# Delta net weights loaded ahead and in parts, zero experts added last, indexed return of the GELU experts' rows

## The reference, cut to what matters

```
x = x + 0.5 * zero_moe(layernorm(x))      # stage 0: 8 routed experts of width 128 + 4 "zero" experts, top 2
x = x +       attention(layernorm(x))     # stage 1
x = x + 0.5 * zero_moe(layernorm(x))      # stage 2: as stage 0
x = x + 0.5 * gelu_moe(layernorm(x))      # stage 3: 8 experts of width 1024, top 2
x = x +       delta_net(layernorm(x))     # stage 4: gated delta rule, 16 key heads, 32 value heads of 128
x = x + 0.5 * gelu_moe(layernorm(x))      # stage 5: as stage 3

zero_moe:  out = sum_e w[e] * down_e(silu(gate_e x) * up_e x) + x * sum(w[zero experts])
gelu_moe:  out = sum over the two picks of w * (gelu(x W1_e + b1_e) W2_e + b2_e)
delta_net: qkvz = x W_qkvz; causal conv of 4 taps and silu on q, k, v; chunks of 64; ...; out = core W_out
```

## Time and profile before

| What | Value |
|---|---|
| median of three runs | 2405.76 us (2404.11 to 2411.33) |
| the profiled execution | 2403.5 us, its span 2401.8 us |
| TensorE busy | 2025.8 us, 84% |
| VectorE busy | 1286.1 us, 54% |
| ScalarE busy | 1000.3 us, 42% |
| GpSimd busy | 391.6 us, 16% |
| mean granted TensorE clock | 0.924 of full speed |

### The profile page before, as it was taken

How to read it: one execution, slowest core, us unless ns; L and a number is a source line. 1 busy time by engine, 2 the same in 40 slices (tenths; PEclk the granted TensorE clock), 3 DMA queues, 4 the chain that set the end, 5 groups by cost and what they waited for, 6 DMA issues and landing times. The chain is left out here.

```text
span 2401.8 us, 52328 instructions
## 1 busy us (share of the span) xinstructions
PE 2025.8 (84%) x20606; PEld 1490.4 (62%) x20606; DVE 1286.1 (54%) x2928; ACT 1000.3 (42%) x2476; POOL 391.6 (16%) x442
## 2 busy tenths in 40 slices
PE   7889898788626689999999999999999998858884
PEld 4544455677514467767776776777677667638774
DVE  4435444212234576777667767766776776431222
ACT  2114421222113445664665566556546654512221
POOL 0002100200200122212221222122122212202102
PEclk9969998899856899999999999999999999958997
DMA  1100003710101111011101110110111010045001
GB/s 46 33 13 1 15 26 105 250 31 21 44 11 45 30 31 24 18 35 24 33 20 37 24 33 20 33 27 18 35 24 33 20 28 11 11 164 187 27 21 62
DMA packets 148345, 100.08 MB, mean 42 GB/s; under 512 B 88640, under 2 KB 134992, under 8 KB 148112
## 3 DMA queue, kind: packets, MB, share of 16 engines
q1 hardware_dynamic: 144368, 86.59, 12.8%
q0 software_dynamic: 3744, 10.23, 1.5%
HBM read 83.28 MB, written 13.50 MB: 40 GB/s over the span
## 5 line engine op out<-in xcount | busy, mean ns | idle before, releaser
L1589 PE MATMUL dn_ps<-xnT,dn_w 128*128 128x512 f32 x512 | 260.5, 635 | 35.2 <-DMA dn_w<-in_W_qkvz_dram 23.9
L1942 DVE SCALAR_TENSOR_TENSOR dn_cv<-dn_raw,dn_cw,dn_cv 128x1024 f32<-128x1024 f32 x192 | 270.6, 1409 | 1.2
L588 PE MATMUL g_ps<-g_w,xnT 128*128 (+1 forms) x736 | 166.1, 379 | 0.0
L1589 PEld LDWEIGHTS dn_ps<-xnT,dn_w 128*128 128x128 f32 x512 | 91.2, 197 | 116.3 <-issue 100.1
L577 PE MATMUL g_ps<-g_xT,g_w_now 128*128 128x128 f32 x960 | 117.4, 282 | 50.3 <-DVE g_w_now L716 50.3
L1734 PE MATMUL dn_ps<-dn_wout,dn_oT 128*128 128x256 f32 x512 | 150.0, 418 | 6.2 <-ACT dn_oT L1749 3.7
L1749 ACT ACTIVATE dn_kdk<-dn_ps,dn_cf 128x128 f32<-128x128 f32 x256 | 80.2, 364 | 179.3 <-PE dn_ps L1629 179.3
L516 ACT ACTIVATE xnT<-g_ps,g_b_now 128x128 f32<-128x128 f32 x240 | 68.6, 368 | 206.1 <-PE g_ps L577 206.1
L577 PEld LDWEIGHTS g_ps<-g_xT,g_w_now 128*128 128x128 f32 x960 | 112.6, 196 | 61.5 <-issue 61.5
L588 PEld LDWEIGHTS g_ps<-g_w,xnT 128*128 128x128 f32 x736 | 136.4, 190 | 16.7
L1749 ACT ACTIVATE dn_raw<-dn_ps 128x512 f32<-128x512 f32 x128 | 76.6, 598 | 148.7 <-PE dn_ps L1589 148.7
(11 more groups left out here) (309 smaller groups left out, 4413.2 us busy)
## 6 DMA issues: line engine op xcount, KB each, us to landing
g_w<-in_fc_dram SPq DMA_DIRECT2D x32, 1024.0 KB, 13.1
dn_w<-in_W_qkvz_dram SPq DMA_DIRECT2D x16, 768.0 KB, 4.5
dn_x<-dn_cum_rows SPq DMA_DIRECT2D x32, 256.0 KB, 3.9
ys_rows<-g_ys SPq DMA_DIRECT2D x46, 128.0 KB, 1.7
dn_wout<-in_W_out_dram SPq DMA_DIRECT2D x16, 256.0 KB, 2.8
f_gate<-in_gateT_dram SPq DMA_DIRECT2D x16, 128.0 KB, 2.2
f_up<-in_upT_dram SPq DMA_DIRECT2D x16, 128.0 KB, 2.4
f_down<-in_downT_dram SPq DMA_DIRECT2D x16, 128.0 KB, 2.4
```

The costliest lines, as they stand in the source:

```text
L588: last = pe.matmul(y_b[i % 2][:, 0:D], hT[i % 2][:, f, :], of(f), start=(f == 0), stop=(f == NF - 1))
L1589: mm = pe.matmul(to, w[:, k, W_COL[u] * P:(W_COL[u] + 1) * P], m.xnT[:, k, b * T:(b + 1) * T], start=(k == 0), stop=(k == KD - 1))
L1942: ins = nc.vector.scalar_tensor_tensor(out=cv[:, u], in0=raw[:, u, :, tap:tap + T], scalar=cw[:, g, tap:tap + 1], in1=cv[:, u], op0=ALU.mu ...
```

## The change

1. `top_two`: the 8 MAX8 follow one another with one wait, then the 8 FIND_INDEX8 with one wait.
2. `moe_zero`: the 8 additions of `xn * zero_w` stand after the experts' loop.
3. `moe_gelu`: VectorE's loop has `copy_w1(i + 1)` first. The tile's result goes to `ys_rows` by an indirect DMA of GpSimd (`put_back`), each row straight to the row of its token and pick; all slots without a token go to one spare row, 2048. Each `put_back` waits for the one before to have landed. When all have landed, SyncE loads the rows back with 16 plain DMAs of 128 KB. `place_u` now comes out of the routing matmuls by a third column group of `token`. The four bias additions stand ahead of the sixteen additions.
4. `delta_net`: the first head's `w`, `cw`, `wout` and all constants are issued in the gates' stage (`load_first`); later heads' q, k and v columns (512 KB) are loaded once `proj` 7 of the head before is done, the z columns (256 KB) once `proj` 11 is.

```diff
@@ top_two
-        chain(nc.vector.max(m8[:, t, :], scores[:, t, :]))
-        chain(nc.vector.max_index(ix[:, t, :], m8[:, t, :], scores[:, t, :]))
+        nc.vector.max(m8[:, t, :], scores[:, t, :]).then_inc(chain.sem, 1)
+    chain.n += NT
+    chain.eng.wait_ge(chain.sem, chain.base + chain.n)
+    for t in range(NT):
+        nc.vector.max_index(ix[:, t, :], m8[:, t, :], scores[:, t, :]).then_inc(chain.sem, 1)
...
@@ moe_zero, vector
-            for t in range(NT):
-                nc.vector.scalar_tensor_tensor(out=m.x[:, t, :], in0=m.xn[:, t, :], scalar=zero_w[:, t:t + 1],
...
-            dve.wait_ge(chain_sem, chain.n + NT)
+            dve.wait_ge(chain_sem, chain.n)
...
+            dve.wait_ge(acc_done, 2 * UNITS * STEPS + A_FREE)
+            for t in range(NT):
+                nc.vector.scalar_tensor_tensor(out=m.x[:, t, :], in0=m.xn[:, t, :], scalar=zero_w[:, t:t + 1],
...
@@ moe_gelu, sync
-            for i in range(TILES):
-                sp.wait_ge(y_copied, i + 1)
-                sp.dma_start(tile_rows(ys_rows, i), ys[:, i % 3, :]).then_inc(ys_stored[i % 3], 16)
+            sp.wait_ge(y_copied, TILES)
             for n in range(3):
                 sp.wait_ge(ys_stored[n], 16 * ((TILES - n + 2) // 3))
+            for t in range(NT):
+                for r in range(2):
+                    sp.dma_start(gathered[r][:, t, :], tile_rows(ys_rows, r * NT + t)).then_inc(ys_back[t], 16)
@@ moe_gelu, gpsimd
+            def put_back(i):
+                pool.wait_ge(y_copied, i + 1)
+                if i >= 1:
+                    pool.wait_ge(ys_stored[(i - 1) % 3], 16 * ((i + 2) // 3))
+                nc.gpsimd.indirect_dma_start(ys_rows, bass.IndirectOffsetOnAxis(ap=place_u[:, i:i + 1], axis=0),
+                                             ys[:, i % 3, :], None).then_inc(ys_stored[i % 3], 16)
+
+            for i in range(RING):
+                fetch(i)
             pool.wait_ge(place_ready, 1)
...
+            for i in range(TILES):
+                if i + RING < TILES:
+                    fetch(i + RING)
+                put_back(i)
@@ moe_gelu, tensor and vector: routing
-            pe.wait_ge(token_ready, 2)
+            pe.wait_ge(token_ready, 3)
...
+            nc.vector.tensor_tensor(token[:, :, 2, :], in_tile[:], over_tiles(route[:, R_BACK:R_BACK + 2 * NT]), ALU.mult).then_inc(token_ready, 1)
...
-            chain(nc.vector.scalar_tensor_tensor(out=place_f[:], in0=tile_f[:], scalar=float(P), in1=slot[:], op0=ALU.mult, op1=ALU.add))
-            nc.vector.tensor_copy(place_u[:], place_f[:]).then_inc(place_ready, 1)
...
+            chain(nc.vector.scalar_tensor_tensor(out=place_f[:], in0=in_tile[:, 0, :], scalar=float(SPARE), in1=in_tile[:, 1, :],
+                                                 op0=ALU.add, op1=ALU.add))
+            nc.vector.tensor_tensor(place_u[:], place_f[:], in_tile[:, 2, :], ALU.subtract).then_inc(place_ready, 1)
@@ moe_gelu, vector: the loop
             for i in range(TILES):
+                if E1 <= i + 1 < TILES:
+                    copy_w1(i + 1)
                 if i + 2 < TILES:
                     copy_x(i + 2)
                 if i >= 1:
                     copy_y(i - 1)
-                if E1 <= i + 1 < TILES:
-                    copy_w1(i + 1)
             copy_y(TILES - 1)
@@ delta_gates, sync (behind its own loads)
+            first = load_first(sp, first_loaded)
...
+            sp.wait_ge(first_loaded, 16 * first)
@@ delta_net
+        def load_first(sp, first_loaded):
+            sp.dma_start(w[:], weights_of(0)).then_inc(first_loaded, 16)
+            sp.dma_start(cw[:], taps_of(0)).then_inc(first_loaded, 16)
+            sp.dma_start(wout[:], out_of(0)).then_inc(first_loaded, 16)
...
             def load_weights(kh):
+                wait(sp, "pj", kh * 12 - 4)
+                sp.dma_start(w[:, :, 0:4 * P], weights_of(kh)[:, :, 0:4 * P]).then_inc(w_loaded, 16)
+
+            def load_z_weights(kh):
                 wait(sp, "pj", kh * 12)
-                sp.dma_start(w[:], W_qkvz[:, kh * NCOL:(kh + 1) * NCOL].rearrange("(k p) n -> p k n", p=P)).then_inc(w_loaded, 16)
+                sp.dma_start(w[:, :, 4 * P:NCOL], weights_of(kh)[:, :, 4 * P:NCOL]).then_inc(wz_loaded, 16)
```

More of the change, by code:

```diff
@@ L342 @@
 R_PART, R_TILE = R_SLOT + P, R_SLOT + P + 1
-R_WIDTH = R_TILE + 2 * NT
+R_BACK = R_TILE + 2 * NT
+R_WIDTH = R_BACK + 2 * NT
+SPARE = 2 * NTOK
 def route_constants():
@@ L359, in route_constants @@
     tile = np.tile(P * np.arange(NT), 2).astype(np.float32)
+    back = (SPARE - NTOK * (np.arange(2 * NT) // NT)).astype(np.float32)
     spread = lambda a: np.broadcast_to(a, (P, len(a)))
     part = r[:, None].astype(np.float32)
-    return np.ascontiguousarray(np.concatenate([before, ones, groups, count, spread(rows), part, spread(tile)], axis=1))
+    return np.ascontiguousarray(np.concatenate([before, ones, groups, count, spread(rows), part, spread(tile), spread(back)], axis=1))
 def moe_gelu(nc, m, tag, gate, gate_bias, fc1, fc1_b, fc2, fc2_b, alpha, iota_in, route_in, xn_rows, ys_rows):
@@ L481, in _, with fetch @@
             pool.wait_ge(tokens_ready, 1)
-            for i in range(TILES):
+            def fetch(i):
                 if i >= RING:
@@ L544, in _ @@
                     pe.wait_ge(in_slot_ready, j // 4 + 1)
-                last = pe.matmul(y_b[0][:, 0:2 * TILES], in_slot[:, j, :], token[:, j].rearrange("p a n -> p (a n)"),
+                last = pe.matmul(y_b[0][:, 0:3 * TILES], in_slot[:, j, :], token[:, j].rearrange("p a n -> p (a n)"),
                                  start=(j == 0), stop=(j == 2 * NT - 1))
@@ L731, in _ @@
                     copy_y(i - 1)
-                if E1 <= i + 1 < TILES:
-                    copy_w1(i + 1)
             copy_y(TILES - 1)
+            for g in range(4):
+                dve.wait_ge(b2_ready, g + 1)
+                two = m.x[:, 2 * g:2 * g + 2, :].rearrange("p t d -> p (t d)")
+                nc.vector.tensor_tensor(two, two, h_b[g], ALU.add).then_inc(b2_added, 1)
             for t in range(NT):
-                if t % 2 == 0:
-                    dve.wait_ge(b2_ready, t // 2 + 1)
-                    two = m.x[:, t:t + 2, :].rearrange("p t d -> p (t d)")
-                    nc.vector.tensor_tensor(two, two, h_b[t // 2], ALU.add).then_inc(b2_added, 1)
                 dve.wait_ge(b2_added, t // 2 + 1)
@@ L1154, with delta_gates @@
 (K_BETA, K_NBETA, K_CUM, K_NGE, K_GE, K_KD, K_GL) = range(7)
-def delta_gates(nc, m, tag, W_ba, A_log, dt_bias, table, cf, cum_rows):
+def delta_gates(nc, m, tag, W_ba, A_log, dt_bias, table, cf, cum_rows, load_first):
     with ExitStack() as ctx:
@@ L1430, in delta_net @@
         w16, w16t = (sb(n, [P, NBC, C]) for n in ("w16", "w16t"))
-        mz = [sb(f"mz{n}", [P, C]) for n in range(LEVELS)]
         four = lambda name, n=P: [sb(f"{name}{s}", [P, B, n]) for s in range(4)]
@@ L2086, in build @@
         load_inputs(nc, m, a["x"], const(a["c_table"], C_EYE))
-        xn_rows, ys_rows = (nc.dram_tensor(f"{n}_rows", (rows, D), F32).ap() for n, rows in (("xn", NTOK), ("ys", SLOTS)))
+        xn_rows, ys_rows = (nc.dram_tensor(f"{n}_rows", (rows, D), F32).ap() for n, rows in (("xn", NTOK), ("ys", SPARE + P)))
         for s in stages:
```

83 lines of the change are left out of this document (47 added, 36 removed).

## The result

The changed kernel took **2319.03 us** in the median of 4 runs (2318.72 to 2321.54), the kernel before on the same chip 2404.94 us (2401.44 to 2411.33, 4 runs). The ratio is 0.9642, with a 95% interval of 0.9621 to 0.9664: faster by 3.6%. 2320.6 us had been predicted, with a range of 2308 to 2348. The total agrees; the terms do not all, and that is what the rest of this document is about.

A forecast was written before the change was run, and what follows sets the result against it. TensorE was taken to lose its time in waits in the GELU stages, chiefly 50.3 us for VectorE's weight copy. The terms summed to -85.2 us, from 2405.8 to 2320.6 us, range 2308 to 2348.

The forecast's parts named there:

- Weight copy first: GELU loop: TensorE's waits for VectorE's weight copy all go, -50.3 us; first such tiles regain the clock, -3.1 us.
- The owner's register load: GELU loop: loading the owner register, 0.30 us and well ahead of its product, does not delay TensorE; nothing.
- Routing: GELU routing: the third part of `token` adds 0.55 us a stage with nothing hiding it, +1.1 us, between 0 and +2.
- End of the GELU stages: Indexed stores and plain loads replace fetching rows back at the stage's end: -9.7 us a stage, -19.4 in all.
- Zero experts: SwiGLU stages: head gains 3.38 us, additions return 3.26 at the end; -0.2 us in all, between -1 and +1.
- Gates' stage: The ten loads issued there come behind the gates' own on the same queue: nothing, or at most +1 us.
- Delta net's start: First head's loads no longer delay TensorE and `dn_x` comes earlier: -5.3 us, between -4 and -7.
- Later heads: Delta net: earlier weight loads remove TensorE's 10.4 us of waits for `dn_w`: -8 us, between -2 and -12.
- gives nothing beyond its start: Rival: in the delta net the next wait moves up, so later heads gain nothing; 2328.6 us, chance 0.08.
- the prediction's last sentence: Sign of error: GELU loop keeps its period, or another delta net wait grows by what `dn_w` gives back.
- The put-backs as the bound: Rival: in the GELU loop each indexed store's landing sets the tile's period; slower, 2475 us at 10 us landing, chance 0.02.
- a late put-back: Rival: indexed stores land after 6.6 us, losing 12 us of the gain at the GELU stages' ends; 2332.6 us, chance 0.14.

The follow-up runs named there:

- experiment 1: Kernel before, with one edit: in the GELU loop the next tile's weight copy stands first; 2345.16 us, ratio 0.9738.
- experiment 2: Changed kernel with the old GELU stage put back (plain stores, 16 indexed gathers, two-part token table) except the new copy order; 2338.05 us, ratio 0.9712.
- experiment 5: Changed kernel with the eight zero-expert additions back ahead of the SwiGLU loop, batched `top_two` kept; 2317.23 us, ratio 0.9622.
- experiment 4: Changed kernel, but SyncE waits until the gates' own loads have landed before issuing the first delta head's loads; 2317.56 us, ratio 0.9620.
- experiment 3: Changed kernel with later delta heads' q, k, v and z weights loaded together again, after the last of twelve projections; 2325.53 us, ratio 0.9653.
- experiment 7: Changed kernel with every indexed store issued twice, the second after the first has landed; 2334.54 us, ratio 0.9695.

## Why the prediction was right, and where it was wrong

- **Weight copy first, -50.3 and -3.1.** Right in its mechanism, too small in size: 61 us in the two stages (experiment 1), not 53.4. The step that failed is the price of one wait. I took the idle time in the row, 1.63 us, and a period of 9.1 - 1.63 = 7.5. But two groups of matmuls that need no wait overlap: the second matmuls are busy for 3.62 us, and the next group starts 3.45 us after them (546.95 to 550.40). The wait cost the 1.63 us and this overlap of 0.17, and the matmuls behind it were longer by 0.08 (3.81 us, now 3.73): 1.87 a tile. The period of the tiles with a fixed owner, 7.24 us, stood in the trace of before and would have told it. Fifteen waits a stage, each some 0.25 us dearer than its row, are the missing 3.8 us; the clock's part came as said, the first such tile's products taking 3.7 us where they took 5.36, at a mean granted clock of 0.70 before (499.0 to 504.4 us) and 1.00 now.
- **The owner's register load, put at nothing.** Right. The period now equals that of the tiles which load no register, so no such load stands in TensorE's path. The Trainium skill gives about 600 ns as the floor of a `tensor_load` ("DMA: Bandwidth & Descriptors", section "Latency and other measured facts"); the trace records 0.30 us for each of TensorE's. No run here shows what a load costs whose value is needed at once.
- **Routing, +1.1.** Right in the profile: TensorE starts on the first tile 0.7 us later after the stage's start (37.9 to 38.6), against +0.55. In stage 3 this start lies at 37.5 to 37.9 us in the three profiles with a two-part table (before, experiments 1 and 2) and at 38.5 to 38.8 in the other nine. The total cannot show a term of this size: the first 32 products behind it alone take 5.7 us in the profile of before and 6.3 in that of experiment 1, whose routing is the same.
- **End of the GELU stages, -19.4.** Right: -9.85 from the last tile's first matmuls to the next stage in stage 3 and -10.4 in stage 5 (43.8 to 33.4), and -15 to -19 in the total of experiment 2, which also holds the routing. Its steps: the last store starts 0.7 us after its copy, 0.3 had been said, and what holds it is not settled (the one before it lands just as the copy ends, at 608.83 + 3.1 = 611.9); SyncE's issue comes 3.3 us after the store's, against a landing put at 3.6. The additions bind as said, with short waits for the loads.
- **Zero experts, -0.2.** Right for stage 0 as a whole (0.0), but not in its halves. "The half of this edit that moves the additions costs what it brings" is wrong: with the selection batched only 1.78 us of the 3.38 were left to gain (experiment 5), against 3.26 at the end, so the move cost 1.9 us more than it brought, and the batching paid for it. In stage 2 it is +2.7, of which this edit is not the cause. TensorE's first groups there are

```profile
302.25 7.00 PE L257 MATMUL f_ps<-f_cls,xnT 128*128 128x12 f32 x32 [0.47 <-ACT xnT L137]
```

  in the changed kernel, but in experiment 4, whose program is the same up to there,

```profile
301.88 5.26 PE L257 MATMUL f_ps<-f_cls,xnT 128*128 128x12 f32 x32 [0.47 <-ACT xnT L137]
```

  and 5.29 us before. Stage 2 then takes 107.6 us in experiment 4 and 107.75 before, but 110.46 in the changed kernel and 111.4 in experiment 1, which runs the code of before. It goes with the execution, not with the edit: the granted clock from 301.9 to 309.4 us was 0.50 of full speed in the changed kernel, its lower level (1.2 GHz), and 0.63 in the same stretch of experiment 4.

  Experiment 1 shows one thing more that the removed wait could cost. Timeline of TensorE in its stage 0:

```profile
36.17 3.78 PE L272 MATMUL f_ps<-f_down,f_h 128*128 128x256 f32 x8 [2.82 <-DVE f_h L313]
39.74 3.15 PE L263 MATMUL f_ps<-xnT,f_gate 128*128 128x512 f32 x4
```

  The granted clock was 1.00 ahead of this wait and 0.50 from 36 to 41 us, and the two groups took 3.1 us more than the 1.99 and 1.88 us that they take in the profile of before, where the clock stayed at 1.00 after a wait of 3.38 us. Stage 0 is 112.7 us there, for 109.7. In stage 2 of experiment 1 the same happened for 1.7 us. In the ten profiles with the batched selection it never did. The prediction has no term for this; with two profiles of the old order its size stays open.
- **Gates' stage, "nothing, or at most +1".** This is the step that was wrong. "The ten loads in the gates' stage come behind the gates' own on the same queue": they do, and still the vector ahead of them landed 3.6 us later (experiment 4). With 1.3 us more for the small matmuls and 0.2 of rest, the stretch from the stage's start to the delta net's block grew from 57.6 to 62.8 us, 5.2 us where at most 1 had been allowed. Why the small matmuls took longer is open: 6.55 us in the changed kernel, 5.28 in experiment 5, which has the same code there, and 6.69 in experiment 4, without the loads behind the vector.
- **Delta net's start, -5.3.** The first projection comes 2.0 us after the block's start instead of 8.8, -6.7 us; behind it the first head keeps its pace, for its next long wait, 14.0 and 13.1 us for `dn_w16t`, ends 65.7 us after the first projection in both kernels. The low end of -4 to -7 was right. With the term above, the loads in the gates' stage brought 1.6 us net.
- **Later heads, -8.** Too large: the forecast and the rival in which the delta net "gives nothing beyond its start" each hold about half. It is about -3.6 (the means under experiment 3), which lies inside the stated -2 to -12. The 10.4 us were one execution's; 5.1 and 5.7 us stood in two others. About as much waits for `dn_wv` now: the prediction's last sentence had named that as the sign that it was wrong, and the wait grew from 26.6 to 32.7 us. Since these two nearly cancel, the runs do not show where the 3.6 us come from.
- **The put-backs as the bound, 0.02, and a late put-back, 0.14.** Both fell, by the landing of 2.5 us and by experiment 7.

## What to carry to other kernels

Take the price of a removed wait from the period of a place in the same trace that has no such wait, not from the idle time of the row; and the size of a sum of small waits from two traces, since one had twice what two others showed. A load that is moved to an idle stage is not free because it is issued last: see which transfer of small packets is still under way on its queue, and who waits for it. Where work has to go somewhere, look for idle time inside a loop (the two additions a step) rather than weigh one end of it against the other.

## What the runs showed of the hardware

- The gates' four vector loads have 4 KB each, in small packets: 4,496 packets under 512 B moved from 666 to 695 us in the kernel before. Right behind them SyncE took 3.88, 4.34 and 5.00 us to issue three loads that took 0.38, 0.47 and 1.64 us once the vectors had landed (experiment 4), and the last vector landed 3.6 to 4.0 us later than with nothing issued behind it.
- An indexed store of 128 rows of 1 KB lands after 2.4 to 4.7 us, median 2.5, faster than the indexed fetch of the same size (3.6 in the earlier trace rows). The last stores of each stage, whose rows all go to the one spare row, took 3.1. Two in a row with a fetch take under 5.1 us of GpSimd's time in a tile.
- The length of an unchanged SwiGLU stage of some 110 us differs between executions: 107.75 and 111.4 us in stage 2 with the old code, 107.6 and 110.5 with the new. Part of it is when TensorE's first groups reach full speed (5.3 or 7.0 us for the same 32 matmuls, at a mean granted clock of 0.63 or 0.50), part a fall of the clock to 0.50 behind waits of 2.8 and 3.5 us in experiment 1, which did not come behind two waits of 3.4 us in the profile of before. A difference of under 4 us in this kernel therefore needs the stage where it arises, not the total.
